# Scores read from PSUM, fewer routing steps, unread products on PE, and sums tile by tile in a fused two-layer graph and expert kernel

## The reference

```python
x = x + _L0_gnn_ref(_layernorm(x), adj, ...)   # softmax over neighbours of leaky_relu(src_i + dst_j), times h
x = x + _L0_ffn_ref(_layernorm(x), ...)        # top 2 of 8 experts, 128 -> 512 -> 128, gelu
x = x + _L1_gnn_ref(_layernorm(x), adj, ...)   # the same attention, relu of the result
x = x + _L1_ffn_ref(_layernorm(x), ...)        # top 2 of 8 experts, 128 -> 256 -> 128, gelu
```

## Time and profile before

| | us |
|---|---|
| median of 3 runs | 965.69 |
| lowest and highest run | 958.6, 968.75 |
| the profiled execution | 966.77 |
| its span, first to last instruction | 964.9 |

### The profile page before, as it was taken

How to read it: one execution, slowest core, us unless ns; L and a number is a source line. 1 busy time by engine, 2 the same in 40 slices (tenths; PEclk the granted TensorE clock), 3 DMA queues, 4 the chain that set the end, 5 groups by cost and what they waited for, 6 DMA issues and landing times.

```text
span 964.9 us, 23945 instructions
## 1 busy us (share of the span) xinstructions
PE 688.7 (71%) x6353; PEld 562.8 (58%) x6384; DVE 734.9 (76%) x2554; ACT 499.7 (52%) x1129; POOL 556.4 (58%) x544
## 2 busy tenths in 40 slices
PE   3877788550999999999977878987305777777600
PEld 2655466450999999998455656776204655566400
DVE  6678988752899999998478888887544788788628
ACT  2556655410777777775146655556304655555334
POOL 0036777775376677767100766666772777777720
PEclk9978977855999999999987777668657999999855
DMA  8373333332233323326432444222232333333757
GB/s 220 110 168 111 104 96 97 91 98 73 67 94 86 87 81 85 88 78 174 142 103 82 132 141 140 86 83 67 69 116 73 103 107 96 96 100 102 234 224 315
DMA packets 129397, 111.45 MB, mean 116 GB/s; under 512 B 30306, under 2 KB 112681, under 8 KB 129352
## 3 DMA queue, kind: packets, MB, share of 16 engines
q1 hardware_dynamic: 112072, 77.04, 28.6%
q0 software_dynamic: 17280, 33.87, 10.7%
HBM read 60.32 MB, written 52.36 MB: 117 GB/s over the span
## 4 chain that ended last, share of the span: by engine, by line
PE 32%; DVE 25%; issue 19%; POOL 12%; ACT 6%; DMA 4%; SPq 1%; POOLq 1%; DVEq 1%; ACTq 0%
PE bank L628 9%; PE bank L642 9%; POOL row_buf L456 6%; POOL y_buf L464 5%; PE bank L519 5%; DVE stat L906 3%; PE bank L516 3%; ACT xn L703 2%; PE bank L500 2%; DMA y_buf<-g_y,g_dst 2%; DVE xin L977 2%; DVE yin L969 2%; DVE x1w L996 2%; PE bank L614 2%; DVE e_msk L956 1%
## 5 line engine op out<-in xcount | busy, mean ns | idle before, releaser
L456 POOL DMA_INDIRECT row_buf<-pay,slot x256 | 264.0, 1031 | 233.4 <-DVE slot L1070 155.2
L464 POOL DMA_INDIRECT y_buf<-g_y,g_dst x284 | 292.2, 1029 | 135.9 <-issue 86.1
L808 ACT ACTIVATE g_xT<-bank 128x512 f16<-128x512 f16 x142 | 84.9, 598 | 167.4 <-PE bank L614 165.2
L628 PE MATMUL bank<-g_xT,w 128*128 128x256 f16 x1278 | 169.0, 279 | 1.7 <-ACT g_xT L808 1.0
L628 PEld LDWEIGHTS bank<-g_xT,w 128*128 x1278 | 118.8, 100 | 20.9 <-issue 2.8
L614 PE MATMUL bank<-ident,g_in 128*128 128x128 f16 x568 | 57.4, 225 | 84.6 <-DMA g_in<-row_buf 73.4
L815 ACT ACTIVATE xn<-bank,b_cols 128x256 f32<-128x256 f32 x216 | 86.8, 474 | 23.9 <-PE bank L628 16.0
L642 PE MATMUL bank<-w,g_h 128*128 x1260 | 85.7, 221 | 18.9 <-DVE g_y L1218 18.7
L642 PEld LDWEIGHTS bank<-w,g_h 128*128 128x128 f16 x1260 | 76.8, 98 | 28.4 <-issue 26.3
L815 ACT ACTIVATE xt<-bank,b_cols 128x256 f32<-128x256 f32 x210 | 84.4, 475 | 15.7 <-PE bank L628 12.1
L614 PEld LDWEIGHTS bank<-ident,g_in 128*128 128x128 f16 x568 | 37.2, 100 | 92.9 <-issue 72.1
(11 more groups left out here) (194 smaller groups left out, 1365.2 us busy)
## 6 DMA issues: line engine op xcount, KB each, us to landing
g_in<-row_buf SPq DMA_DIRECT2D x142, 130.0 KB, 2.2
yin<-y_buf SPq DMA_DIRECT2D x20, 512.0 KB, 5.3
x_buf<-x1w SPq DMA_DIRECT2D x16, 520.0 KB, 5.2
xin<-x_buf SPq DMA_DIRECT2D x10, 520.0 KB, 4.3
y_buf<-g_y,g_dst POOLq DMA_INDIRECT x284
xin<-in_x_dram SPq DMA_DIRECT2D x8, 512.0 KB
adj_in<-in_adj_dram SPq DMA_DIRECT2D x16, 256.0 KB, 3.6
row_buf<-pay,slot POOLq DMA_INDIRECT x256, 2.6
```

Of the source, the lines that this page charges most:

```text
L456: pool.indirect_dma_start(row_buf[L][:, :], bass.IndirectOffsetOnAxis(ap=slot[q][:, k, t:t + 1], axis=0), pay[q][:, t, :], None).then_inc( ...
L464: pool.indirect_dma_start(y_buf[L][:, :], bass.IndirectOffsetOnAxis(ap=g_dst[k][:, t:t + 1], axis=0), g_y[k][:, t, :], None, bounds_check= ...
L628: last = nc.tensor.matmul(dst, w[:, bass.ds(e * (2 * HID[L]) + (wp * HID[L] + c * P), P)], g_xT[q][:, xp, :], start=(m == 0), stop=(m == 2))
L808: nc.scalar.activation(g_xT[q][:, :, :], x_ps[q], ACT.Copy).then_inc(s.gT_sb, 1)
```

## The change

- **Scores.** ACT's copy is gone. DVE reads bank 2 and masks first, with the mask divided by the slope, then applies the leaky relu.
- **Routing.** Column 129 of the payload holds 8 minus the expert (which the routing has anyway), and the groups compare with `grp_m`, 8 minus theirs. Token numbers stay in the payload tiles and are raised by two blocks at each use, so the running count `tok_run` is gone. Two products become one instruction. Between the layers DVE waits for all scatters of layer 0 and files the new numbers.
- **Sums in layer 1.** `arrive` adds the first result to x by eight fused instructions, `take_in` the second, and `add_attention` scales and adds in eight. In both layers `arrive` of block n+2 stands ahead of `scores` of block n+1, except in the first step.
- **PE.** In layer 1 PE waits for the input statistics and issues eight more unread products in a step. Ahead of the groups of each layer it issues 96, after it has tables and weights and POOL has begun its last block.
- **Groups.** SP loads the registers of its first four loads before it waits for the scatters. DVE finishes group 0 before it places and splits group 2.

```diff
+SLOPE = 0.2
-IDLE_START, IDLE_LOOP = 112, 8
+IDLE_START, IDLE_LOOP, IDLE_ST1, IDLE_GROUPS = 112, 8, 8, 96
@@ SP, groups
+                early = [sp.value_load(grp_ri[0:1, k:k + 1], min_val=0, max_val=ROWS - GRP) for k in range(AHEAD)]
                 for q in range(2):
                     sp.wait_ge(s.scattered[q], 16 * TOP * TILES * NBLK // 2)
...
-                    load_group(k, k)
+                    load_group(k, k, early[k])
@@ PE, blocks
                     keep_busy(IDLE_ATT[L])
+                    if L == 1 and not last:
+                        pe.wait_ge(SL[L].st1, n + 2)
+                        keep_busy(IDLE_ST1)
@@ PE, groups
                 pe.wait_ge(s.tables, 1)
                 pe.wait_ge(w_ready[L], 1)
+                es = experts(0, 2)
+                pe.wait_ge(pool_turns, L * (NBLK + NG) + NBLK)
+                with pe.Fori(0, IDLE_GROUPS // IDLE_LOOP):
+                    keep_busy(IDLE_LOOP)
                 for k in range(2):
                     to_feature_rows(k, 0)
-                es = experts(0, 2)
@@ ACT, blocks
-                    if not last:
-                        copy_scores(L, n + 1)
@@ DVE
+            def file_under(numbers):
+
+                for q in range(2):
+                    last = V.tensor_scalar(pay[q][:, :, D], numbers, float((q - 2) * BLK), None, ALU.add)
+                return last
...
-                dve.wait_ge(s.e_copied, n + 1)
-                ch.did(V.scalar_tensor_tensor(e_act[:, :], e_sb[:, :], 0.2, e_sb[:, :], ALU.mult, ALU.max))
-                ch.wait()
-                ch.did(V.scalar_tensor_tensor(e_msk[:, :], keep[:, :], MASKED[L], e_act[:, :], ALU.add, ALU.min))
+                dve.wait_ge(s.e_ps, n + 1)
+                ch.did(V.scalar_tensor_tensor(e_msk[:, :], keep[:, :], MASKED[L] / SLOPE, bank[2][:, :], ALU.add, ALU.min))
+                ch.wait()
+                ch.did(V.scalar_tensor_tensor(e_act[:, :], e_msk[:, :], SLOPE, e_msk[:, :], ALU.mult, ALU.max))
...
+            def add_result(q, k):
+
+                for t in range(TILES):
+                    last = V.scalar_tensor_tensor(xin[q][:, t, X_AT:X_END], yin[q][:, k, t, :], xin[q][:, t, k:k + 1],
+                                                  xin[q][:, t, X_AT:X_END], ALU.mult, ALU.add)
+                return last
...
                 if L == 1:
-                    weights = xin[q][:, :, 0:TOP].rearrange("p t k -> p k t").unsqueeze(3).to_broadcast([P, TOP, TILES, D])
-                    ch.did(V.tensor_tensor(yin[q][:, :, :, :], yin[q][:, :, :, :], weights, ALU.mult))
+                    ch.did(add_result(q, 0))
...
-                    for k in range(TOP):
-                        ch.wait()
-                        ch.did(V.tensor_tensor(xin[q][:, :, X_AT:X_END], xin[q][:, :, X_AT:X_END], yin[q][:, k, :, :], ALU.add))
+                    ch.wait()
+                    ch.did(add_result(q, 1))
...
-                    ch.did(V.tensor_tensor(h_new[:, :, :], h_new[:, :, :],
-                                           rinv[:, :].unsqueeze(2).to_broadcast([P, TILES, D]), ALU.mult))
-                    ch.wait()
-                    last = V.tensor_tensor(x1w[q][:, :, X_AT:X_END], h_new[:, :, :], xin[q][:, :, X_AT:X_END], ALU.add)
+                    for t in range(TILES):
+                        last = V.scalar_tensor_tensor(x1w[q][:, t, X_AT:X_END], h_new[:, t, :], rinv[:, t:t + 1],
+                                                      xin[q][:, t, X_AT:X_END], ALU.mult, ALU.add)
...
-                V.tensor_copy(pay[q][:, :, D], tok_run[:, :])
+                V.tensor_scalar(pay[q][:, :, D], pay[q][:, :, D], 2.0 * BLK, None, ALU.add)
...
-                        V.tensor_scalar(tok_run[:, :], tok_run[:, :], float(BLK), None, ALU.add)
-                        V.tensor_scalar(pay[q][:, :, D + 1], r1[:, :], -1.0, float(NE), ALU.mult, ALU.add)
...
-                for k in range(TOP):
-                    V.tensor_tensor(hot_pos[:, k, :, :], hot[:, k, :, :], pos[:, :, :], ALU.mult)
+                V.tensor_tensor(hot_pos[:, :, :, :], hot[:, :, :, :], pos[:, :, :].unsqueeze(1).to_broadcast([P, TOP, TILES, NE]), ALU.mult)
@@ DVE, blocks
-                    if not (last or over):
+                    if first:
                         scores(L, n + 1)
                     if not (before_last or last or over):
                         arrive(L, *block_at(i, d + 2))
+                    if not (first or last or over):
+                        scores(L, n + 1)
@@ DVE, groups
                         g, a = SPAN * i + k, (k + 2) % AHEAD
+                        very_first = isinstance(g, int) and g == 0
+                        if very_first:
+                            finish(0, 0, 0, es[0])
                         if not last or k + 2 < n:
                             place(g + 2, a, per_turn * i + (k + 2) // AHEAD)
                             split(g + 2, a)
-                        finish(g, k % AHEAD, per_turn * i + k // AHEAD, es[k])
+                        if not very_first:
+                            finish(g, k % AHEAD, per_turn * i + k // AHEAD, es[k])
@@ DVE, between the layers
                 blocks(L)
                 if L == 0:
                     V.memset(h_sb[:, :, H_END:H_END + 1], 1.0)
-                    ch.did(V.tensor_copy(tok_run[:, :], cst[:, C_TOK:C_TOK + TILES]))
+                    for q in range(2):
+                        dve.wait_ge(SL[0].scattered[q], 16 * TOP * TILES * NBLK // 2)
+                    ch.did(file_under(cst[:, C_TOK:C_TOK + TILES]))
                 group_tables(L)
                 split_first(L)
                 groups(L)
```

More of the change, by code:

```diff
@@ L227, in gnn_moe_kernel @@
         past_n = sb("past_n", [P, NG, NE])
-        grp_e, grp_b, grp_c, grp_r = (sb(n, [P, NG]) for n in ("grp_e", "grp_b", "grp_c", "grp_r"))
+        grp_e, grp_m, grp_b, grp_c, grp_r = (sb(n, [P, NG]) for n in ("grp_e", "grp_m", "grp_b", "grp_c", "grp_r"))
         grp_ei, grp_ri = sb("grp_ei", [P, NG], I32), sb("grp_ri", [P, NG], I32)
@@ L734, in input_columns @@
                 copy_transposed(n, SL[L].xT_ps, xnT, SL[L].xT_sb)
-            def copy_scores(L, n):
-                s = SL[L]
-                act.wait_ge(s.e_ps, n + 1)
-                nc.scalar.activation(e_sb[:, :], bank[2][:, :], ACT.Copy).then_inc(s.e_copied, 1)
             def copy_features(L, n):
@@ L869, in _ @@
             V.tensor_copy(tri16[:, :], cst[:, C_TRI:C_TRI + P])
-            ch.did(V.tensor_scalar(tok_lane[:, :], cst[:, C_TOK:C_TOK + 1], TILES - 1.0 / P, None, ALU.mult))
+            ch.did(V.tensor_scalar(tok_lane[:, 0:1], cst[:, C_TOK:C_TOK + 1], TILES - 1.0 / P, None, ALU.mult))
             ch.wait()
-            V.tensor_scalar(tok_run[:, :], cst[:, C_TOK:C_TOK + TILES], 1.0 / P, tok_lane[:, 0:1], ALU.mult, ALU.add)
+            ch.did(V.tensor_scalar(tok_lane[:, 1:], cst[:, C_TOK:C_TOK + TILES], 1.0 / P, tok_lane[:, 0:1], ALU.mult, ALU.add))
+            ch.wait()
+            file_under(tok_lane[:, 1:])
             for L in range(2):
@@ L1023, in route @@
                 yield
-                for k, (val, vmax, eq, cand, cmax) in enumerate(((lg, l_max, eq1, ca, r1), (lg2, l_max2, eq2, cb, r2))):
-                    ch.did(V.tensor_reduce(vmax[:, :], val[:, :, :], AX_X, ALU.max))
+                for k, (val, vmax, eq, cand, cmax) in enumerate(((lg, l_max[:, :], eq1, ca, pay[q][:, :, D + 1]), (lg2, l_max2[:, :], eq2, cb, r2[:, :]))):
+                    ch.did(V.tensor_reduce(vmax, val[:, :, :], AX_X, ALU.max))
                     yield
-                    ch.did(V.tensor_tensor(eq[:, :, :], val[:, :, :], bc(vmax[:, :]), ALU.is_equal))
+                    ch.did(V.tensor_tensor(eq[:, :, :], val[:, :, :], bc(vmax), ALU.is_equal))
                     yield
@@ L1146, in group_tables @@
                 V.tensor_scalar(grp_ei[:, :], grp_e[:, :], float(NE - 1), None, ALU.min)
+                V.tensor_scalar(grp_m[:, :], grp_e[:, :], -1.0, float(NE), ALU.mult, ALU.add)
                 ch.did(V.scalar_tensor_tensor(grp_b[:, :], grp_c[:, :], float(GRP), grp_r[:, :], ALU.mult, ALU.add))
```

24 lines of the change are left out of this document (11 added, 13 removed).

## The result

| | before | after |
|---|---|---|
| median | 964.62 us (20 runs) | 971.73 us (20 runs) |
| lowest and highest run | 957.4, 971.23 | 966.63, 973.54 |
| the profiled execution | 966.77 | 971.66 |
| its span | 964.9 | 969.8 |

What follows compares the result with a forecast made beforehand. First layer: POOL bounds the graph stage, PE the groups; second: the loop through DVE, then POOL. 27.2 - 21.6 - 2.1 = +3.5 us on 966.8 gives 970.3, less 1.1 for the median: 969, range 959 to 983.

Steps and rivals of the forecast that it cites:

- The wait in layer 0: Layer 0's last seam: DVE waits for scatters, landing at 231.3, ahead of tables and weight split; 14.5 us to the weights.
- The 96 products: Unread products ahead of each layer's groups: 22.3 us, all on the path in layer 0; bounds 20.6 to 41.
- Scores from PSUM: DVE's read of scores from PSUM costs nothing extra; the dropped ACT copy gains 0.63 us where DVE waits.
- Layer 1's step: Second graph stage: 3.1 us less a period, 22.8 for 25.9: 2.23 of waiting, 0.63 fused sums, 0.24 routing.
- the step of 660.74: Kernel before, layer 1: ACT waited 2.64 us for scores, not 5.31, because the clock had stayed up.
- Before the first slots of layer 1: Start of the second graph stage: 6.1 us saved (bounds 3.4 and 6.5), 2.7 of it from block 1's full clock.
- Layer 1's groups: Second layer's groups: PE starts 0.9 us later, full clock and DVE's reorder gain 3.0, net -2.1 us.
- From span to median: Whole execution: the median is 1.1 us below the profiled execution, so 970.3 becomes 969.
- (B): Layer 1's steps: DVE's arrival waits for its x load, 2 us in each of five: 979; chance 0.20.
- (C): Layer 1's sums: fused instructions cost 0.2 us each, saving 1.8 us more a step: 962; chance 0.13.
- (D): Ahead of the groups: clock stays at 1.2 GHz through the 96 products, 19 us more per layer: 1007; chance 0.05.
- (E): First layer's wait costs nothing because something else resets the tiles in time: near 937; chance 0.03.

Runs made afterwards that it cites:

- the block-wide kernel: The kernel after with layer 1's sums block-wide as in the kernel before, in place of 24 fused 128x128 instructions: 976.7 us, 1.012 of before.
- the kernel with both edits: The kernel after with scores ahead of the arrival again and without layer 1's eight products per step: 979.81 us, 1.016 of before; second time 977.78 us.
- the four kernels above: The kernel after with reset behind the weight split (944.92 us), without the 96 products (953.98), late reset with 56 and 80 products (934.95), late reset without products (937.88).
- the late reset: The kernel after with layer 0's wait for scatters and reset moved behind group tables and weight split: 944.92 us, 0.981 of before.
- the three kernels: The kernel after with scores ahead of the arrival again (973.25 us), without layer 1's eight products per step (975.35), and with both (979.81).

## Why the prediction was right, and where it was not

- **The wait in layer 0.** Landing 231.3 predicted, 230.87 measured; 14.5 us to the weights, 14.04 measured. Right, in mechanism and size, and confirmed from both sides: taking it off the path gives 26.8 us, adding it alone to the kernel before delays the transposes by 18.0 (without the products the loads end last, 6.1 us behind the weights; the prediction had 5).
- **The 96 products.** 22.3 predicted, 22.7 measured, though the register loads and the hop ahead of them took 1.5 us and not 0.3. Transposes 268.4 predicted, 269.08 measured. The pipeline's fill gave back the 2.3 taken: first output 7.5 us behind the transposes, 9.8 before. But not all of it is the clock, as the prediction had it: without the products it was 8.7. Layer 0 in sum +27.2 predicted, +27.6 to +28.5 measured, by the row chosen.
- **Scores from PSUM.** Nothing predicted; 0.68 us, the same as from SBUF.
- **Layer 1's step.** 3.1 us a period predicted, 3.4 measured against that profile, and the number hides a wrong step; that it fits is luck in which execution was profiled. The sum put the 2.23 us down to the order of scores and arrival. By the second profile of the kernel before, 2.3 of the 3.4 belong to the clock: the old step runs at 23.54 when the clock stays up between transposes and scores. What the change takes from DVE's own work is 1.1 (23.54 less 22.46), of which the block-wide kernel measures 0.66 for the sums, and the rest, 0.4, is put down to the dropped routing steps and what else DVE no longer does, which no run took alone; it is inside the 0 to 0.5 given. Against the second profile of the kernel before the span grew by 11.3 us (958.5 to 969.8), not by 4.9. What order and products are worth is safety: with both undone the loop has again a path of 24.6 us, and with both in place 20 runs lie within 7 us where the kernel before spreads over 14. The row with the sign of it was in the prediction itself: the step of 660.74, where the same chain took half as long, and that step of the kernel before had no wait ahead of its scores.
- **Before the first slots of layer 1.** 6.1 predicted; 531.33 became 553.78, 22.5 later, behind a layer 0 that was 28.5 late at DVE's first work in layer 1: 6.1. The 2.7 us in it for the clock in block 1's step is borne out, 2.4 us by the kernel after without the eight products and 3.3 by the kernel before with them, though not in every execution: the kernel with both edits waited 4.0 us there in its first profile and 0.9 in its second. At block 5's slots the shift was 5.6 predicted and 5.4 measured, at the transposes 6.5 and 6.3.
- **Layer 1's groups.** The gain of 3.0 was over-sized. The first result came 4.1 us sooner behind the transposes (7.06 us, where the earlier trace rows gives 11.17), but POOL then took 185.6 us to its last issue, where it took 183.0, with small waits for DVE such as 1.13 us ahead of its second group. Left are 1.6 of 3.0, which is the 1.4 us by which the span grew more than forecast (4.9, not 3.5).
- **From span to median.** I took 1.1 us off as the distance of the profiled execution from the median. The kernel before was profiled in one of its long executions, 2.2 over the median of 20; the kernel after shows no long path (none in its profile, nor in those of the four kernels above that leave the steps of its layer 1 as they are), and its profile is its median. So the medians lie 7.1 us apart where the spans are 4.9 apart, and 969 became 971.7.
- **Rivals.** (B) fell, but narrowly: DVE never waits for a load of x in the steady steps, yet the one issued at 595.87 took 4.3 us to land, at 600.2, and DVE came at 600.5. Its remark that stores and scatters share the DMA queues holds for the queue of stores and loads only: the profile has the scatters on another, q0, beside q1. (C) fell: the fused instructions took 2.19 us. (D) fell: 22.7 us at 0.90 of the clock. (E) was not there, and the late reset shows what it would have been worth if one makes it so: 945 us and not 937, since the 96 products then end last; with them gone or fitted it is 938 and 935.

What stays open: whether the first two of the three kernels (order alone, products alone undone) also have long paths; their medians say a little, their profiles show none. What puts an execution on the long path, since the length of the pause alone does not sort the steps: in the kernel with the wait alone, 1.7 us ahead of the routing products at 661.69 was followed by the wait at 671.41, while 1.75 us in the kernel before was not. And whether unread products ahead of the groups, once hidden, are worth their place.

## What to carry to other kernels

A wait goes to the last place in an engine's queue where it is needed: the same wait for the same scatters cost 27 us ahead of the group tables and nothing behind them. Work that is only there to keep a clock up has to end when the real input lands, and here even then it earned 3 us at most in the steps between the stages. The cheap place for it was a pause inside a loop: eight products a round, which cost nothing there, took away the long path. And where a loop's time depends on where a clock falls, take a second profile of the kernel before you say what an edit gained: two executions of the kernel before differed by up to 13.8 us, and the change moved the median by 7.1.

## What the runs showed of the hardware

- One program's steady loop has two periods, 25.8 and 23.5 us, with the same instructions in both. The long one goes with a granted clock of 0.50 between transposes and scores, after TensorE's idle time ahead of the routing products, the short one with 1.00; eight products in that idle time left only the short one in 12 runs. Five periods on the long path cost 11.7 us, which is a large part, not all, of the spread from 953 to 974 us. The mean granted clock goes with it: of 19 executions timed together, the five shortest (956 to 960) had 0.839 to 0.850, the five longest (970 to 971) 0.827 to 0.834. An execution can change path on its way (651.48 in the kernel with both edits).
- An indirect issue of POOL takes 0.95 to 1.15 us beside DVE's 128-element instructions (126 of 128) and up to 2.4 us beside a 2.3 us one with two SBUF inputs (2.7 in the second profile of the kernel before). The Trainium skill ("SBUF — State Buffer", section "SBUF: two separate sides") says that such an instruction and a GpSimd operation that reads SBUF exclude each other: whichever starts first has the port for its whole length. The row at 603.44 fits that, ending 0.8 us behind the DVE instruction's end at 605.01. That the short instructions leave gaps for the issue is an inference.
- 96 products of 128x512 take 22.4 and 22.7 us in the two places, after idle times of TensorE of 14 and 37 us, at a mean granted clock of 0.91 and 0.90; 112 at a clock of 1.00 took 24.0.
- A VectorE instruction of 128x512 f32 with one input in PSUM took 0.68 us, with both in SBUF 0.69.
